# Grouped attention: one VectorE operation makes the row maxima of two neighbouring banks, and the eight PSUM banks become two tensors of four

## The reference

```python
# 32 query heads of 8 channels, 8 key heads; keys and values are ctx (4 x 256 x 64)
qh = q.reshape(B, S, KV, G, D).transpose(0, 2, 3, 1, 4)
kh = k.reshape(B, S, KV, D).transpose(0, 2, 1, 3)
scores = jnp.einsum('bkgsd,bktd->bkgst', qh, kh) / scale
weights = jax.nn.softmax(scores, axis=-1)
out = jnp.einsum('bkgst,bktd->bkgsd', weights, vh)
```

## Time and profile before

| | |
|---|---|
| median of 3 runs | 983.55 us (978.01 to 986.1) |
| the profiled execution | 984.03 us |
| its span, first to last instruction | 982.2 us |
| outside the span | 1.8 us |
| TensorE matmul busy | 870.8 us (89%) |
| VectorE busy | 643.3 us (65%) |
| ScalarE busy | 383.9 us (39%) |
| GpSimd busy | 358.9 us (37%) |
| mean granted TensorE clock | 0.955 of 2.4 GHz |

### The profile page before, as it was taken

How to read it: one execution, slowest core, us unless ns; L and a number is a source line. 1 busy time by engine, 2 the same in 40 slices (tenths; PEclk the granted TensorE clock), 3 DMA queues, 4 the chain that set the end, 5 groups by cost and what they waited for, 6 DMA issues and landing times.

```text
span 982.2 us, 13012 instructions
## 1 busy us (share of the span) xinstructions
PE 870.8 (89%) x4643; PEld 652.0 (66%) x4668; DVE 643.3 (65%) x1378; ACT 383.9 (39%) x828; POOL 358.9 (37%) x393
## 2 busy tenths in 40 slices
PE   6897675988999998889999998888999998789997
PEld 5675344754787786744787886653788786426886
DVE  6332799795355998895355999875355999764333
ACT  4111743326236443426326443417226544243111
POOL 5202485120042875220043875220042876000322
PEclk9897877999999999999999999979999999879999
DMA  6204000002023330301024330302022330300452
GB/s 217 110 0 175 0 1 0 1 14 98 1 81 113 126 113 2 107 29 82 1 81 145 97 111 1 108 1 110 1 68 69 94 109 17 108 1 1 129 153 84
DMA packets 22196, 67.69 MB, mean 69 GB/s; under 512 B 2860, under 2 KB 4780, under 8 KB 21492
## 3 DMA queue, kind: packets, MB, share of 16 engines
q1 hardware_dynamic: 21876, 66.80, 20.8%
q10 hardware_dynamic: 256, 0.07, 0.0%
HBM read 65.74 MB, written 1.05 MB: 68 GB/s over the span
## 4 chain that ended last, share of the span: by engine, by line
PE 49%; DVE 19%; POOL 12%; issue 12%; ACT 7%; DMA 1%; ACTq 1%; POOLq 0%; DVEq 0%; SPq 0%
PE B L779 22%; PE F L779 21%; POOL arena L465 7%; DVE arena L1430 5%; DVE nmx L1501 3%; PE B L1068 3%; POOL spare L550 2%; ACT big L746 2%; POOL arena L475 2%; PE F L808 1%; DVE arena L1270 1%; DVE arena L1442 1%; PE F L790 1%; POOL rs L447 1%; PE B L1149 1%
## 5 line engine op out<-in xcount | busy, mean ns | idle before, releaser
L779 PE MATMUL B<-spare,mw 128*128 128x256 f32 x880 | 209.3, 382 | 0.0
L779 PEld LDWEIGHTS B<-spare,mw 128*128 128x128 f32 x880 | 166.5, 191 | 24.8 <-issue 2.6
L550 POOL TENSOR_TENSOR spare<-q_t 128x256 f32<-128x256 f32 x112 | 82.0, 738 | 193.3 <-DVE q_t L1567 134.2
L1430 DVE TENSOR_TENSOR_SCAN arena<-F,arena 128x512 f32<-128x512 f32 x128 | 149.5, 1207 | 3.7 <-ACT F L702 2.3
L465 POOL TENSOR_TENSOR arena<-du,arena 128x1024 f32<-128x1024 f32 x60 | 140.9, 2360 | 9.8 <-PE F L779 8.5
L702 ACT ACTIVATE F<-delta,a_neg 128x255 f32<-128x255 f32 x256 | 109.9, 467 | 72.6 <-DVE arena L1430 72.6
L779 PE MATMUL B<-mw,spare 128*128 128x256 f32 x448 | 115.4, 381 | 1.2 <-POOL spare L550 1.2
L779 PE MATMUL F<-arena,ident 128*128 128x256 f32 x400 | 105.1, 406 | 1.4 <-POOL arena L475 1.0
L768 ACT ACTIVATE q_t<-B 128x256 f32<-128x256 f32 x112 | 42.0, 381 | 159.2 <-PE B L779 152.6
L1562 DVE SCALAR_TENSOR_TENSOR q_t<-q_t,B 128x256 f32<-128x256 f32 x112 | 46.6, 416 | 77.7 <-ACT q_t L768 77.4
L779 PEld LDWEIGHTS B<-mw,spare 128*128 128x128 f32 x448 | 84.2, 190 | 15.9 <-POOL spare L550 3.9
(11 more groups left out here) (228 smaller groups left out, 1284.0 us busy)
## 6 DMA issues: line engine op xcount, KB each, us to landing
mw<-in_w_moe SPq DMA_DIRECT2D x112, 384.0 KB, 3.1
room<-in_w_f SPq DMA_DIRECT2D x4, 2544.0 KB, 9.1
room<-in_w_l SPq DMA_DIRECT2D x4, 768.0 KB, 7.1
w_m<-in_w_m SPq DMA_DIRECT2D x1, 2112.0 KB
room<-in_w_l SPq DMA_DIRECT2D x4, 512.0 KB, 4.9
x_t<-in_x_t SPq DMA_DIRECT2D x4, 256.0 KB, 3.3
x_tok<-in_x_tok SPq DMA_DIRECT2D x4, 256.0 KB, 6.4
y<-x SPq DMA_DIRECT2D x4, 256.0 KB, 2.2
```

The lines of the kernel that those rows point to most:

```text
L550: g.tensor_tensor(hid1[0:r, m % HID_RING, :], hraw[0:r, m % 3, :], crs[0:r, int(m >= MTE), :], ALU.mult)\
L779: return t_.matmul(dst, lhsT, rhs, start=start, stop=stop, skip_group_check=True)
L1430: v.tensor_tensor_scan(h, F[i][:, :], h, 0.0, ALU.mult, ALU.add)\
```

## The change

The eight PSUM tensors become two of four banks each, and F and K are lists of views of them. A new helper max_banks gives the two neighbouring banks of a phase as one operand of 2 banks x 2 heads x 256 scores, and one reduction of 1024 elements per partition takes the place of two of 512. It writes the same four places of nmx. The step `mx{n}` is now stepped once per phase. The matmuls, the waits and their order, and all other operations stay.

```diff
-        F = [ctx.enter_context(nc.psum_tensor(f"F{i}", [P, 512], F32)) for i in range(4)]
-        K = [ctx.enter_context(nc.psum_tensor(f"B{i}", [P, 512], F32)) for i in range(4)]
+        banks_f = ctx.enter_context(nc.psum_tensor("F0", [P, 2048], F32))
+        banks_k = ctx.enter_context(nc.psum_tensor("B0", [P, 2048], F32))
+        F = [banks_f[:, 512 * i:512 * i + 512] for i in range(4)]
+        K = [banks_k[:, 512 * i:512 * i + 512] for i in range(4)]
...
+        def max_banks(b, n):
+
+            half = slice(1024 * (n % 2), 1024 * (n % 2) + 1024)
+            return (banks_f if b == B - 1 and n >= 8 else banks_k)[:, half].rearrange("p (i v t) -> p i v t", i=2, v=2)
...
                     dve.wait_ge(*pb.at(f"ms{n}", b))
-                    for i in range(2):
-                        v.tensor_reduce(nmx[:, s, g // 4, :, 2 * (g % 4) + i], two(max_bank(b, n, i)),
-                                        AX_X, ALU.max, negate=True).then_inc(db.step(f"mx{n}"), 1)
+                    j = 2 * (g % 4)
+                    v.tensor_reduce(nmx[:, s, g // 4, :, j:j + 2].rearrange("p v i -> p i v"), max_banks(b, n),
+                                    AX_X, ALU.max, negate=True).then_inc(db.step(f"mx{n}"), 1)
```

## The result

The changed kernel has a median of 975.84 us over 20 runs (974.91 to 980.34). Twenty runs of the kernel before beside it have 983.54 us (977.83 to 987.9). The ratio is 0.994 with a 95% interval of 0.9924 to 0.9956: 7.7 us (0.8%) lie between the medians and 6.0 (0.6%) between the means of the twenty runs. The forecast was 980.4 us, a gain of 3.2. The time lies in the range and the sign is right, but the gain is about twice the forecast (2.4 times by the medians, 1.9 by the means), and the range reached down to it only because it had been drawn to the rival without a drop of the clock.

What follows compares the result with a forecast made beforehand. TensorE and VectorE were taken to bound bm0 to bm7, VectorE alone bm8 to bm13. Three interleaved items at 0.9 us (2.7) plus 0.5 in the last gave 3.2: 983.55 to 980.4 us, range 975.0 to 986.0.

Steps and rivals of the forecast that it cites:

- The price of a pair: VectorE, each pair of banks: one reduction lasting 1.22 us, 1.13 start to start instead of 1.21; 0.075 us saved per pair.
- bm0 to bm7 in the interleaved items: Items 1 to 3, both engines full: eight pairs free 0.60 us of VectorE; gain between 0.27 and 0.60, taken as 0.45.
- bm8 to bm15: Items 1 to 3, VectorE without a gap: two branches gain 0.30 and 0.60 us; 0.45 taken per item.
- the front's extra share: Items 1 to 3: VectorE's own line to ve and xp gains all eight pairs, 0.60 us, against 0.30 for the back.
- The branch of mx11: Items 1 to 3, bm13's matmuls, ScalarE's square and TensorE's queue: gains only the pairs bm8 to bm11, 0.30 us.
- The last back: Last item, TensorE at half clock: 0.36 us from bm0 to bm7 and 0.15 from bm9 and bm15, sum 0.5 us.
- the loop of two: Last item, bm0 to bm7: TensorE and VectorE alternate, period (1.20 + 1.13) / 2 = 1.165 us, saving 0.045 per pair.
- rival 2: TensorE's clock: without the third interleaved item's half-clock drop of 4.84 us, 975.5 us, chance 0.17; one more drop, 985.2, chance 0.12.
- the three signs: Wrong if reduction exceeds 1.30 us, item period isn't 0.6 to 1.2 us shorter, or granted clock changes more than path.
- Rival 3: VectorE: the wide reduction restarts at the bank's boundary or each row, costing 0.06 us more per pair; 987.4 us, chance 0.09.
- rival 1: The gain is swallowed by full TensorE, a transfer or an unmoved neighbour; time stays at 983 to 984 us, chance 0.13.

Runs made afterwards that it cites:

- the experiment with n < 8: Changed kernel with wide reductions only in bm0 to bm7 of all items, two reductions per pair in bm8 to bm15: 977.94 us, ratio 0.9964.

## Why the prediction was right, and where not

**The price of a pair: right.** 1.22 us and a distance of 1.13 were forecast from line 1442; 1.219 and 1.13 were measured. Four dimensions and two banks cost nothing. The saving of 0.125 us per pair, worked out from the cycle table of the Trainium skill ("VectorE: DVE Perf Modes", the section on the trn2 errata), did not appear; it was 0.08. Nor does that table give the durations here, as the prediction had supposed: they are 0.68 and 1.22 us against its 0.658 and 1.192.

**bm0 to bm7 in the interleaved items: too high.** The prediction took 0.45 us. Measured from bm0 to bm8: 208.22 - 195.00 = 13.22 us before, 208.97 - 195.88 = 13.09 after, 0.13 us. The step that failed was to count the waits of TensorE's weight loads (0.54 and 0.26 us) as time to be won. The timeline of TensorE's loads after, beside the earlier trace rows:

```profile
203.65 0.11 PEld L786 LDWEIGHTS B<-k_t,q_t 128*128 128x128 bf16 x2 [0.43 <-DVE nmx L1508]
...
206.69 0.73 PEld L786 LDWEIGHTS F<-arena 128*128 128x128 f32 x4 [0.23 <-DVE arena L1290]
```

The waits are 0.11 and 0.03 us shorter, but the time in which no matmul runs fell only from 0.27 us to 0.20 in the stretch: a load overlaps the matmul in front of it, and most of its wait was hidden there. My own lower bound had been 0.27, the uncovered time of the stretch, and even that was not reached; the experiment with n < 8 gives 0.08 per period.

**bm8 to bm15: the right branch, but the front's extra share was lost.** The branch of mx11, ScalarE's square and TensorE's queue was put at 0.30. bm13's matmuls start at 214.02 and bm0 at 195.88:

```profile
214.02 0.38 PE L786 MATMUL B<-k_t,q_t 128*128 128x512 bf16 x1 [0.75 <-DVE nmx L1508]
...
220.37 0.88 DVE L1310 SCALAR_TENSOR_TENSOR xp<-F,rs,x_tok 128x256 f32<-128x256 f32 x2 [0.82 <-POOL rs L454]
```

18.14 us from bm0, against 18.46 before: 0.32 less in all, of which 0.19 here. It is 0.19 and not 0.30 because of a wait that I overlooked: bm9's matmuls stand behind bn0's copy on ScalarE, and VectorE, now done with bm8 sooner, waits for them. bm9's reduction starts 1.28 us after bm8's (210.25 in the chain, 208.97) instead of 1.21. xp gained 0.45 us (24.94 to 24.49), not the 0.9 that I named, and of this the period kept only 0.30, which is what the branch of TensorE and the back had gained (0.32). Taking the mean of the two branches was the mistake; the numbers fit the later one setting the period, though no run separates the branches. Items 1 to 3 gave 0.9 us where the prediction had 2.7.

**The last back: right in kind.** In the kernel with wide reductions only there, the loop of two at half clock was 1.17 us per pair, forecast 1.165, and the eight pairs took 9.42 us instead of 9.74, forecast 9.4. The changed kernel's own profile doesn't show this loop, because TensorE had its full clock there:

```profile
849.00:859.00 10.00, 5.03 (x19) 1.17 (x18) 9.53 (x10) 0.00 (x0) 0.00 (x0) 1.00 0.00 0
```

The eight pairs took 9.14 us, 0.6 less than before.

**The clock: the rival that I put beside the forecast made the time.** The sum of the path, some 1.2 to 1.5 us, is half of what was forecast or less. Most of the rest of the 7.7 is rival 2, to which I gave 0.17 with 975.5 us; the time was 975.84. That its number came out so close is luck: its path part of 3.2 us was twice too large, and its 4.84 us for one drop stand against some 5 to 6 between the groups. Some 1.3 us of the 2.7 between the lower groups are explained by neither. Two of the three signs by which the prediction called itself wrong came true: the period shortened by 0.30 us and not by 0.6 to 1.2, and the granted clock changed by more than the path. That the time lies in the range is owed to the rival, and the forecast's own range (978.7 to 982.8) missed it. I had treated the drop as an accident of the profiled run that might go or come. The runs show that it is a state in which the kernel before finds itself in 63 of 104 runs, so that its absence is worth its full price in the median, and that it goes with VectorE's pace (six of twelve at 1.20 us per pair, none of twenty at 1.13, or three by time). The three runs that I had, 978, 983.5 and 986, were the hint: the periods' 4.84 us is most of the 5.5 us between the first two. The reason that I gave, the shorter bm8 to bm13 stretch, is not confirmed. More work there removes the drops, but of the wide reductions those of bm8 to bm15 left them in ten runs of twelve, and those of bm0 to bm7 in four. How that comes about stays open, and so does the part of the moment.

**Rival 3** is refuted by the 1.219 us, and rival 1 holds in part: of the 1.2 us that VectorE saved per item, three quarters were swallowed, by TensorE in the first stretch and by bn0.

## What to carry to other kernels

Merging two VectorE operations that read neighbouring PSUM banks saves the fixed part of one, here 0.075 us of start-to-start distance, and the nearest operation of the doubled size in the trace gives that price beforehand. Before multiplying it, follow every branch to the end and count the latest one only; a wait of a weight load is time to be won only as far as no matmul covers it. And where runs of one kernel lie in two groups, compare the periods inside one trace: if one of them holds a half-clock stretch, ask what share of the runs has it, because a change of 0.3 us in a period of 219 went with a median that moved by the whole distance of the groups.

## What was not expected of the hardware

A memset of one element per partition between two reductions cost 0.015 us of distance, while a copy of one element cost 0.06 to 0.07 (1.145 and 1.19 to 1.20 us against 1.13), though their durations are 0.06 and 0.14 us. And TensorE's granted clock went with 0.075 us per pair: half-clock time of 73 us and more in 63 of 104 runs before, in none of 20 after (three of these still had a smaller drop by their time), and in none of 12 when 12 repeated matmuls, 2.6 us of work in a span of 977, were added to the kernel before.
